# Node-by-edge selections on VectorE: 32-bit output in two edge walks, another element order in layer 2's first pass

## The chip, the cores and the metric

The kernel runs on one core of one Trainium2 chip. Its time is the device time of one execution in microseconds; the median of three executions is compared.

## What is computed

Four graph layers run one after the other over 6250 nodes of 128 features and 100000 edges sorted by destination. Each layer normalises the nodes, passes messages along the edges and adds its result to the nodes.

```python
h = jnp.maximum(_layernorm(x, axis=-1), 0.0);  x = x + _L0_gnn_ref(h, edge_attr_128, src, dst, ...)   # sums over edges
h = jnp.maximum(_layernorm(x, axis=-1), 0.0);  x = x + _L1_gnn_ref(h, edge_index, ...)                # attention, 8 heads
h = jnp.maximum(_layernorm(x, axis=-1), 0.0);  x = x + _L2_gnn_ref(h, edge_index, edge_type_8, ...)   # two relational layers
h = jnp.maximum(_layernorm(x, axis=-1), 0.0);  x = x + _L3_gnn_ref(h, edge_index, ...)                # attention, 2 heads
# attention, per edge: w = q[dst] . k[src];  softmax over the edges of a dst;  agg[dst] += softmax(w) * v[src]
# relational: mean over the edges of one dst and relation of (x @ W[relation])[src], summed over the 8 relations
```

## The kernel before

**Tiles and windows.** The nodes form 50 windows of 128. The sorted edges form up to 832 tiles of 128 edges, each of which belongs to one window; 829 tiles can hold edges. 16 tiles make a step, 52 steps a walk, and 4 tiles a group. `local_d` in DRAM holds, for every edge place, the number of its node inside its window.

**The selection.** From those numbers VectorE makes, for 16 tiles at once, a matrix of nodes by edges: partition n, column (tile, edge) is 1 where the edge's node is n. `make_selt` compares the 2048 numbers, broadcast to all partitions by one DMA on SP's queue, with the partition's own number `g.tile_f[:, 0:1]` (line 1874 in the walks, line 2793 in layer 2's first pass). Numbers and result are bf16; both are double-buffered by step.

**The two attention walks** (layers 1 and 3, `attention_edges`; tiles named l1te and l3te). ScalarE copies the bf16 selection into the 32-bit tile `wide` (`widen`, line 1784), which TensorE uses as weights in `look_up` (line 1671) to fetch each edge's query from its window. VectorE multiplies the queries with gathered rows (`product`), reduces them to scores, runs scans for the segment maximum, weighs the gathered values (`weigh`), and adds the tile sums that TensorE makes with a second selection (`sum_up`, line 1723) to the windows (`add`). Each engine has one written-out order per step: VectorE calls `make_selt(s + 1)` in the middle of step s, between two additions and ahead of `scan_carries`; TensorE looks up groups of step s + 1 at the end of step s; the weighing of a group comes two to three steps after its product.

**The gathers.** GpSimd issues one indirect DMA per tile (line 1627), which brings 128 rows of keys and values from `pair_d`. 48 buffers stand ready; a group of gathers waits for the weighing of 48 tiles before.

**Layer 2's first pass** (`gather_relations`; tiles named l2e). GpSimd gathers a tile of message rows (line 2644, 16 buffers). In `count` (line 2715) TensorE multiplies each tile's 128x128 slice of the selection, as weights, with the inverse counts of its window; from that VectorE makes a coefficient for each edge, and with it, per tile, the matrix for the sums of line 2762.

The last pass of layer 2 (`gather_nodes`; tiles named l2f, gathers in line 854) has no such selection. Nor has layer 0.

Of the kernel before, what the change touches and what calls it, by code (L numbers as in the profile page):

```python
# [5 lines left out]
P = 128  # L6
# [14 lines left out]
S = 16  # L21
NS = T // S
# [7 lines left out]
BF16 = mybir.dt.bfloat16  # L30
I32 = mybir.dt.int32
ALU = mybir.AluOpType
# [1522 lines left out]
def attention_edges(nc, g, sem, name, heads, queries, first, acc, aw, outputs=None):  # L1555
# [4 lines left out]
    GS = S // G  # L1560
# [9 lines left out]
    with Stage(nc, name) as st:  # L1570
        o = outputs(st) if late else None
        rows = g.xh[:, 0:R * 2 * D].rearrange("p (r f) -> p r f", f=2 * D)
        local = st.sb("local", [P, 2, S * P], BF16)
        selt = st.sb("selt", [P, 2, S, P], BF16)
        wide = st.sb("wide", [P, 2, S, P])
        sel = st.sb("sel", [P, V, G, P])
        narrow = st.sb("narrow", [P, 2, P, G], BF16)
# [28 lines left out]
        gathered = [sem(f"{name}_g{r}") for r in range(RG)]  # L1606
        local_in = [sem(f"{name}_local{b}") for b in range(2)]
        mask_in = [sem(f"{name}_mask{b}") for b in range(2)]
        (set_up, selt_made, widened, looked, used, reduced, sel_made, scores_turned, scanned, spread, summarised, carried,
         handed, picked, picked_sum, joined, topped, fell, shifted, firsts, expd, alphad, diagd, ex_turned, alpha_spread,  # L1610
         factored, scaled, weighted, beside, summed, added, taken, chosen, ready, cleared) = (
            sem(f"{name}_{k}") for k in (
                "set_up", "selt", "widened", "looked", "used", "reduced", "sel", "scturn", "scanned", "spread", "summar",
                "carried", "handed", "picked", "picksum", "joined", "topped", "fell", "shifted", "firsts", "expd", "alphad",
                "diagd", "exturn", "alspread", "factored", "scaled", "weighted", "beside", "summed", "added", "taken", "chosen", "ready", "cleared"))

# [3 lines left out]
        with nc.Block() as block:  # L1620
# [9 lines left out]
            @block.sync  # L1630
            def _(sp):
                if late:
                    o.load(sp)
                    o.fetch(sp, 0)
                    o.fetch(sp, 1)
                for s in range(NS):
                    b = s % 2
                    if s >= 2:
                        sp.wait_ge(selt_made, s - 1)
                    sp.dma_start(local[:, b, :], g.local_d[s * S * P:(s + 1) * S * P].partition_broadcast(P)) \  # L1640
                        .then_inc(local_in[b], 16)
                    if s >= 2:
                        sp.wait_ge(fell, s - 1)
                        if first:
                            sp.wait_ge(firsts, s - 1)
                    sp.dma_start(mask[:, b, :, :].rearrange("p k e -> p (k e)"), g.mask_d[s * P:(s + 1) * P, :]) \
                        .then_inc(mask_in[b], 16)
                    sp.dma_start(ends[:, b, :, :], view(g.ends_d.tensor, s * S, [[0, HS], [TA, 2], [1, S]])) \
                        .then_inc(mask_in[b], 16)
                    if late and s >= LAG + 2:  # L1650
                        o.store(sp, s - LAG - 2)
                        o.fetch_after(sp, s - LAG - 2)
                if late:
                    for k in range(NS - LAG - 2, o.EACH):
                        o.store(sp, k)
                        o.fetch_after(sp, k)
                    o.land(sp)
# [119 lines left out]

            @block.scalar
            def _(act):
                def widen(s):  # L1780
                    act.wait_ge(selt_made, s + 1)
                    if s >= 2:
                        act.wait_ge(looked, GS * (s - 1))
                    nc.scalar.copy(wide[:, s % 2, :, :], selt[:, s % 2, :, :]).then_inc(widened, 1)

                def exps(b):
                    act.wait_ge(fell, b + 1)
                    if b >= 1:
                        act.wait_ge(diagd, b)
                    nc.scalar.activation(alpha[:, :], fall[:, :], ACT.Exp).then_inc(alphad, 1)  # L1790
                    act.wait_ge(shifted, b + 1)
                    if b >= 1:
                        act.wait_ge(ex_turned, b)
                    nc.scalar.activation(ex[:, :], low[:, :], ACT.Exp).then_inc(expd, 1)
                    act.wait_ge(alphad, b + 1)
                    if b >= 1:
                        act.wait_ge(alpha_spread, b)
                    nc.scalar.activation(diag[:, 0:HS], g.ident[0:HS, 0:HS], ACT.Copy, scale=alpha[:, 0:1]).then_inc(diagd, 1)

                def take_weights(b):  # L1800
                    act.wait_ge(ex_turned, b + 1)
                    act.wait_ge(alpha_spread, b + 1)
                    if b >= 2:
                        act.wait_ge(beside, GS * (b - 1))
                    kinds = 2 if first else 1
                    nc.scalar.copy(weights[:, b % 2, 0:kinds, :, :], px[b % 2][:, 0:kinds, :, :]).then_inc(taken, 1)

                def widen_choice(n):
                    act.wait_ge(chosen, n + 1)
                    if n >= V:  # L1810
                        act.wait_ge(summed, G * (n - V + 1))
                    nc.scalar.copy(sel[:, n % V, :, :], narrow[:, n % 2, :, :].rearrange("p n t -> p t n")).then_inc(sel_made, 1)  # L1812

                def put_beside(n):
                    b = n // GS
                    act.wait_ge(taken, b + 1)
                    if n >= V:
                        act.wait_ge(summed, G * (n - V + 1))
                    k = n % GS * G
                    if first:  # L1820
                        ins = nc.scalar.copy(ve[:, n % V, :, D:].rearrange("p i (k h) -> p i k h", k=2),
                                             weights[:, b % 2, :, k:k + G, :].rearrange("p k i h -> p i k h"))
                    else:
                        ins = nc.scalar.copy(ve[:, n % V, :, D:], weights[:, b % 2, 0, k:k + G, 0:heads])
                    ins.then_inc(beside, 1)

                act.wait_ge(set_up, 1)
                widen(0)
                for j in range(5):
                    lo, hi = j * NW // 5 * aw, (j + 1) * NW // 5 * aw  # L1830
                    nc.scalar.activation(acc[:, lo:hi].rearrange("p (w f) -> p w f", f=EACH),
                                         g.iota[:, 0:EACH].unsqueeze(1).broadcast_to([P, (hi - lo) // EACH, EACH]),
                                         ACT.Copy, scale=0.0).then_inc(cleared, 1)
                for s in range(NS + 3):
                    b, z, y, k = s - 1, s - 2, s - 3, s - LAG
                    if late and k >= 1:
                        o.squash(act, k - 1)
                    if y >= 0:
                        widen_choice(GS * y + 3)
                        put_beside(GS * y + 3)  # L1840
                    if 0 <= z < NS:
                        widen_choice(GS * z)
                        for j in range(3):
                            put_beside(GS * z + j)
                    if s + 1 < NS:
                        widen(s + 1)
                    if 0 <= z < NS:
                        widen_choice(GS * z + 1)
                    if late and k >= 0:
                        o.share(act, k)  # L1850
                        o.move(act, k)
                        o.shift(act, k)
                    if 0 <= z < NS:
                        widen_choice(GS * z + 2)
                    if 0 <= b < NS:
                        exps(b)
                        take_weights(b)
                if late:
                    o.squash(act, NS + 2 - LAG)
                    for k in range(NS + 3 - LAG, o.EACH):  # L1860
                        o.share(act, k)
                        o.move(act, k)
                        o.shift(act, k)
                        o.squash(act, k)

            @block.vector
            def _(dve):
                windows = {}

                def make_selt(s):  # L1870
                    dve.wait_ge(local_in[s % 2], 16 * (s // 2 + 1))
                    if s >= 2:
                        dve.wait_ge(widened, s - 1)
                    nc.vector.tensor_scalar(selt[:, s % 2, :, :].rearrange("p s e -> p (s e)"), local[:, s % 2, :],
                                            g.tile_f[:, 0:1], None, ALU.is_equal).then_inc(selt_made, 1)

                def choose(n):
                    if n >= 2:
# [723 lines left out]
def gather_relations(nc, g, sem, name, table, index, width, acc, a):  # L2602
# [7 lines left out]
    with Stage(nc, name) as st:  # L2610
# [27 lines left out]
        with nc.Block() as block:  # L2638
# [147 lines left out]
            def _(dve):  # L2786
                c = Chain(dve, dv)

                def make_selt(s):
                    dve.wait_ge(local_in[s % 2], 16 * (s // 2 + 1))  # L2790
                    if s >= 2:
                        dve.wait_ge(counted, s - 1)
                    nc.vector.tensor_scalar(selt[:, s % 2, :, :].rearrange("p s e -> p (s e)"), local[:, s % 2, :],
                                            g.tile_f[:, 0:1], None, ALU.is_equal).then_inc(selt_made, 1)

                def mark(s):
# [197 lines left out]
```

## Time and profile before

| | us |
|---|---|
| median of 3 runs | 6016.26 (6013.54 to 6016.91) |
| the profiled execution | 6008.73 |
| its span, first to last instruction | 6006.7 |
| busy: TensorE / VectorE / GpSimd / ScalarE | 4143.8 / 3868.2 / 4039.4 / 1476.3 |
| mean granted TensorE clock, of full speed | 0.756 |
| gathers: walk 1, layer 2's first pass, its last pass, walk 2 begin at about | 1257, 2708, 3795, 4870 |

PE is TensorE's multiplication, PEld its weight load, DVE is VectorE, ACT ScalarE, POOL GpSimd. A busy share is a mean over stages with different limits, so each stage is read by itself: which engine has no idle time but its own issue, and which wait ends last. In the timeline two instructions of different engines can be set side by side by their start times.

### The profile page before, as it was taken

Reading aid. Unit: us, or ns where it says so; the run is one execution under the profiler, and the core shown is the slowest. Engines: PE = TensorE matmul, PEld = TensorE weight load, DVE = VectorE, ACT = ScalarE, POOL = GpSimd, SP = SyncE. Lnnn points to the kernel's source line nnn. Section 1 sums busy time; section 2 is a strip of 40 time slices with the busy share of each in tenths; the row PEclk is TensorE's granted clock in tenths of the full one; section 3 lists DMA queues with packets and bytes.
Section 4 is the critical chain, followed back from the end, with each engine's and each line's share of the span. In section 5 each row is a group of like instructions: output and inputs, shape, how many; then the busy total and the mean of one; then the engine's idle time right before and its main releaser. Section 6 shows DMA issues by size and latency. Waiting matters only on the chain. (4 is left out here: it accounts for less than half of the span.)

```text
span 6006.7 us, 86021 instructions
## 1 busy us (share of the span) xinstructions
PE 4143.8 (69%) x19030; PEld 3329.8 (55%) x19030; DVE 3868.2 (64%) x11925; ACT 1476.3 (25%) x3938; POOL 4039.4 (67%) x4191
## 2 busy tenths in 40 slices
PE   5678878867777766896878777444444447777776
PEld 4667766656666664444555555333333336666665
DVE  8555555557777777646666666344444447778885
ACT  5122222222222222451111111011111123333332
POOL 2677777757777774007777777577777767777773
PEclk9988888867777776998888888555555567777776
DMA  2544444434444445165454555222222254454443
GB/s 59 145 129 120 117 121 117 120 112 134 134 139 135 138 135 127 58 289 161 153 161 153 156 157 141 61 64 69 63 69 63 69 114 139 143 150 143 144 150 64
DMA packets 426774, 738.44 MB, mean 123 GB/s; under 512 B 100522, under 2 KB 280579, under 8 KB 419700
## 3 DMA queue, kind: packets, MB, share of 16 engines
q0 software_dynamic: 173200, 436.47, 27.6%
q1 hardware_dynamic: 244484, 289.62, 14.7%
q10 hardware_dynamic: 8592, 6.82, 0.4%
q8 instruction: 176, 2.88, 0.2%
q14 instruction: 322, 2.64, 0.1%
HBM read 613.55 MB, written 120.20 MB: 122 GB/s over the span
## 5 line engine op out<-in xcount | busy, mean ns | idle before, releaser
L1627 POOL DMA_INDIRECT xh<-pair_d,src_i x1658 | 1605.5, 968 | 570.6 <-issue 489.0
L2644 POOL DMA_INDIRECT l2e_rows<-msg_d,msg_i x829 | 798.3, 963 | 565.9 <-POOLq L61 313.7
L854 POOL DMA_INDIRECT l2f_rows<-msg_d,msg_i x829 | 785.3, 947 | 288.5 <-issue 241.1
L999 POOL DMA_INDIRECT l0e_rows<-node_d,src_i x829 | 786.7, 949 | 260.6 <-issue 218.3
L1156 PE MATMUL l0e_ps<-l0e_rows,l0e_sel 128*128 128x256 f32 x1664 | 671.6, 494 | 227.7 <-DVE early_acc L1223 90.0
L888 PE MATMUL l2f_ps<-l2f_rows,l2f_sel 128*128 128x128 f32 x1664 | 428.5, 424 | 578.1 <-DVE l2f_sel L907 366.5
L888 PEld LDWEIGHTS l2f_ps<-l2f_rows,l2f_sel 128*128 128x128 f32 x1664 | 373.4, 316 | 660.5 <-DVE l2f_sel L907 406.9
L2762 PE MATMUL l2e_ps<-l2e_rows,l2e_sel 128*128 128x256 f32 x1664 | 534.4, 447 | 187.4 <-DMA l2e_rows<-msg_d,msg_i 145.0
L919 DVE TENSOR_TENSOR xh<-xh,l2f_ps 128x128 f32 x832 | 239.5, 288 | 517.3 <-PE l2f_ps L888 410.6
L1223 DVE TENSOR_TENSOR early_acc<-early_acc,l0e_ps 128x264 f32 x832 | 356.8, 429 | 323.6 <-PE l0e_ps L1157 245.7
L2821 DVE TENSOR_TENSOR l_acc<-l_acc,l2e_ps 128x256 f32 x832 | 349.4, 420 | 304.3 <-PE l2e_ps L2762 300.7
L2762 PEld LDWEIGHTS l2e_ps<-l2e_rows,l2e_sel 128*128 128x128 f32 x1664 | 329.1, 218 | 337.0 <-issue 178.3
L1671 PE MATMUL l1te_pq<-l1t_queries,l1te_wide 128*128 x1664 | 332.2, 362 | 262.9 <-DVE l1te_prod L1890 252.2
L1671 PE MATMUL l3te_pq<-l3t_queries,l3te_wide 128*128 x1664 | 322.2, 354 | 256.4 <-DVE l3te_prod L1890 236.5
L1156 PEld LDWEIGHTS l0e_ps<-l0e_rows,l0e_sel 128*128 128x128 f32 x1664 | 310.7, 230 | 269.1 <-issue 211.5
L1671 PEld LDWEIGHTS l1te_pq<-l1t_queries,l1te_wide 128*128 128x128 f32 x1664 | 287.2, 260 | 309.8 <-issue 309.5
L1671 PEld LDWEIGHTS l3te_pq<-l3t_queries,l3te_wide 128*128 128x128 f32 x1664 | 279.1, 254 | 296.4 <-issue 294.8
L1157 PEld LDWEIGHTS l0e_ps<-l0e_of_rel,l0e_sel 128*128 128x128 f32 x1664 | 386.4, 232 | 74.2
L1723 PE MATMUL l1te_ps<-l1te_ve,l1te_sel 128*128 128x144 f32 x1664 | 373.2, 383 | 11.0 <-DVE l1te_ve L2003 10.8
L2019 DVE TENSOR_TENSOR l1acc_acc<-l1acc_acc,l1te_ps 128x144 f32 x832 | 246.8, 297 | 175.9 <-PE l1te_ps L1723 169.5
L1723 PEld LDWEIGHTS l1te_ps<-l1te_ve,l1te_sel 128*128 128x128 f32 x1664 | 326.5, 270 | 19.6 <-DVE l1te_ve L2003 13.5
L2019 DVE TENSOR_TENSOR l_acc<-l_acc,l3te_ps 128x130 f32 x832 | 234.4, 282 | 155.7 <-PE l3te_ps L1723 151.6
(454 smaller groups left out, 8074.5 us busy)
## 6 DMA issues: line engine op xcount, KB each, us to landing
l0e_rows<-in_edge_attr_dram SPq DMA_DIRECT2D x832, 64.0 KB
msg_d<-l1t_queries SPq DMA_DIRECT2D x50, 1024.0 KB, 3.9
l1te_local<-local_d SPq DMA_DIRECT2D x52, 512.0 KB, 4.8
l2e_local<-local_d SPq DMA_DIRECT2D x52, 512.0 KB
l3te_local<-local_d SPq DMA_DIRECT2D x52, 512.0 KB
xh<-pair_d,src_i POOLq DMA_INDIRECT x1658, 2.8
msg_d<-l2e_msg SPq DMA_DIRECT2D x50, 512.0 KB
l0e_rows<-node_d,src_i POOLq DMA_INDIRECT x829
```

Source lines behind the costliest of these rows:

```text
L854: pool.indirect_dma_start(rows[:, t % R, :], None, table, bass.IndirectOffsetOnAxis(index[:, t:t + 1], 0)) \
L888: nc.tensor.matmul(ps[t % B][:, 0:D], sel[:, n % V, t % G, :], rows[:, t % R, :], start=True, stop=True).then_inc(summed, 1)
L999: pool.indirect_dma_start(rows[:, t % R, 0:D], None, table, bass.IndirectOffsetOnAxis(g.src_i[:, t:t + 1], 0)).then_inc(gathered[t % R], 16)
L1156: nc.tensor.matmul(ps[r % B][:, 0:2 * D], sel[:, r // G % 2, r % G, :], rows[:, r, :], start=True, stop=True)
L1157: nc.tensor.matmul(ps[r % B][:, 2 * D:W0], sel[:, r // G % 2, r % G, :], of_rel[:, r // G % 2, r % G, :], start=True, stop=True).then_inc( ...
L1223: nc.vector.tensor_tensor(one, one, ps[s][:, 0:W0], ALU.add).then_inc(added, 1)
L1627: pool.indirect_dma_start(rows[:, t % R, :], None, g.pair_d, bass.IndirectOffsetOnAxis(g.src_i[:, t:t + 1], 0)).then_inc(gathered[n % RG], 16)
L1671: mm = nc.tensor.matmul(pq[n % 2][:, i * D:(i + 1) * D], wide[:, n // GS % 2, n % GS * G + i, :], queries[:, bass.ds(ws[i] * D, D)], start ...
L1723: nc.tensor.matmul(slot(t), sel[:, n % V, t % G, :], ve[:, n % V, t % G, :], start=True, stop=True).then_inc(summed, 1)
L2019: nc.vector.tensor_tensor(part, part, slot(t), ALU.add).then_inc(added, 1)
L2644: pool.indirect_dma_start(rows[:, t % R, :], None, table, bass.IndirectOffsetOnAxis(index[:, t:t + 1], 0)).then_inc(gathered[t % R], 16)
L2762: nc.tensor.matmul(ps[t % B][:, 0:width], sel[:, t // G % 2, t % G, :], rows[:, t % R, :], start=True, stop=True).then_inc(summed, 1)
```

## The change

In the walks the bf16 tile `selt`, its semaphore and ScalarE's `widen` go. VectorE's comparison writes `wide`, the 32-bit tile, itself, and waits for the lookups that last read that half of `wide`. SP's refill of the edge numbers waits for the same instruction as before, by the semaphore that it now raises. In layer 2's first pass the comparison keeps its tiles, types and place; only the order in which the 2048 columns are read and written changes, from edges inside tiles to tiles inside edges.

```diff
@@ attention_edges
-        selt = st.sb("selt", [P, 2, S, P], BF16)
         wide = st.sb("wide", [P, 2, S, P])
@@ sync
                     if s >= 2:
-                        sp.wait_ge(selt_made, s - 1)
+                        sp.wait_ge(widened, s - 1)
@@ scalar
-                def widen(s):
-                    act.wait_ge(selt_made, s + 1)
-                    if s >= 2:
-                        act.wait_ge(looked, GS * (s - 1))
-                    nc.scalar.copy(wide[:, s % 2, :, :], selt[:, s % 2, :, :]).then_inc(widened, 1)
...
-                widen(0)
...
-                    if s + 1 < NS:
-                        widen(s + 1)
@@ vector
                 def make_selt(s):
                     dve.wait_ge(local_in[s % 2], 16 * (s // 2 + 1))
                     if s >= 2:
-                        dve.wait_ge(widened, s - 1)
-                    nc.vector.tensor_scalar(selt[:, s % 2, :, :].rearrange("p s e -> p (s e)"), local[:, s % 2, :],
-                                            g.tile_f[:, 0:1], None, ALU.is_equal).then_inc(selt_made, 1)
+                        dve.wait_ge(looked, GS * (s - 1))
+                    nc.vector.tensor_scalar(wide[:, s % 2, :, :].rearrange("p s e -> p (s e)"), local[:, s % 2, :],
+                                            g.tile_f[:, 0:1], None, ALU.is_equal).then_inc(widened, 1)
@@ gather_relations, make_selt
-                    nc.vector.tensor_scalar(selt[:, s % 2, :, :].rearrange("p s e -> p (s e)"), local[:, s % 2, :],
+                    nc.vector.tensor_scalar(selt[:, s % 2, :, :].rearrange("p s e -> p e s"),
+                                            local[:, s % 2, :].rearrange("p (s e) -> p e s", s=S),
                                             g.tile_f[:, 0:1], None, ALU.is_equal).then_inc(selt_made, 1)
```

## Rows read from the trace of the kernel before

**Rows 1.** Busy time by stretch: PE, PEld, DVE, ACT, POOL, clock, DMA share, GB/s

```profile
1260.00:2320.00 1060.00, 744.74 (x3781) 656.80 (x3782) 805.76 (x2443) 301.98 (x655) 802.17 (x827) 0.73 0.48 135
2700.00:3760.00 1060.00, 828.91 (x3477) 569.05 (x3476) 691.13 (x1954) 133.93 (x340) 798.31 (x829) 0.86 0.52 155
4870.00:5930.00 1060.00, 750.20 (x4144) 670.60 (x4144) 815.31 (x2622) 344.68 (x878) 795.50 (x824) 0.76 0.50 143
```

**Rows 2.** GpSimd's waits, whole span: total us, times, longest us

```profile
POOL xh L1627 <- issue: 489.0, 1605, 0.3
...
POOL l2e_rows L2644 <- issue: 228.4, 750, 0.3
...
POOL l2e_rows L2644 <- PE l2e_ps L2762: 23.8, 78, 0.3
```

**Rows 3.** The page's groups: count, busy us, mean ns, idle before

```profile
L1627 POOL DMA_INDIRECT xh<-pair_d,src_i x1658 | 1605.5, 968 | 570.6 <-issue 489.0
L2644 POOL DMA_INDIRECT l2e_rows<-msg_d,msg_i x829 | 798.3, 963 | 565.9 <-POOLq L61 313.7
L854 POOL DMA_INDIRECT l2f_rows<-msg_d,msg_i x829 | 785.3, 947 | 288.5 <-issue 241.1
```

**Rows 4.** Waits for gathered rows: 1400 to 2200, 5000 to 5800, 2900 to 3600

```profile
DVE l1te_prod L1890 <- DMA xh<-pair_d,src_i: 40.1, 51, 3.6
...
DVE l3te_prod L1890 <- DMA xh<-pair_d,src_i: 45.8, 37, 2.6
...
PE l2e_ps L2762 <- DMA l2e_rows<-msg_d,msg_i: 96.6, 48, 4.0
```

**Rows 5.** Timeline, five places: start us, duration us, engine, line

```profile
1943.42 0.95 POOL L1627 DMA_INDIRECT xh<-pair_d,src_i  x1 [0.30 <-issue]
1943.43 0.75 DVE L1874 TENSOR_SCALAR l1te_selt<-l1te_local,tile_f 128x2048 bf16<-128x2048 bf16 x1
...
1474.58 1.32 POOL L1627 DMA_INDIRECT xh<-pair_d,src_i  x1 [0.30 <-issue]
1475.03 0.75 DVE L1874 TENSOR_SCALAR l1te_selt<-l1te_local,tile_f 128x2048 bf16<-128x2048 bf16 x1
...
2249.01 0.95 POOL L1627 DMA_INDIRECT xh<-pair_d,src_i  x1 [0.30 <-issue]
2249.50 0.97 DVE L1874 TENSOR_SCALAR l1te_selt<-l1te_local,tile_f 128x2048 bf16<-128x2048 bf16 x1
2250.27 1.02 POOL L1627 DMA_INDIRECT xh<-pair_d,src_i  x1 [0.30 <-issue]
...
1575.66 0.95 POOL L1627 DMA_INDIRECT xh<-pair_d,src_i  x1 [0.30 <-issue]
1576.76 0.75 DVE L1874 TENSOR_SCALAR l1te_selt<-l1te_local,tile_f 128x2048 bf16<-128x2048 bf16 x1
1576.92 1.41 POOL L1627 DMA_INDIRECT xh<-pair_d,src_i  x1 [0.31 <-issue]
...
2874.53 0.94 POOL L2644 DMA_INDIRECT l2e_rows<-msg_d,msg_i  x1 [0.30 <-issue]
2875.67 0.75 DVE L2793 TENSOR_SCALAR l2e_selt<-l2e_local,tile_f 128x2048 bf16<-128x2048 bf16 x1
2875.78 1.45 POOL L2644 DMA_INDIRECT l2e_rows<-msg_d,msg_i  x1 [0.30 <-issue]
```

**Rows 6.** Selection and copy: ns min/median/max, first and last start; who waited, us, times

```profile
L1874 DVE TENSOR_SCALAR l1te_selt<-l1te_local,tile_f x52: 744/748/999, 1259.9 to 2292.8; 128x2048 bf16<-128x2048 bf16 x52
...
L1784 ACT CAST l1te_wide<-l1te_selt x52: 1897/1898/1902, 1261.0 to 2293.7; 128x2048 f32<-128x2048 bf16 x52
...
  PE l3te_pq L1671: 19.5, 2
  PE l1te_pq L1671: 10.5, 1
```

**Rows 7.** Single-input VectorE work of two widths, grouped: busy us, mean ns

```profile
L447 DVE CAST od_lows<-iota 125x2048 bf16<-125x2048 f32 x1 | 1.2, 1200 | 0.0
...
L478 DVE CAST tb_local<-tb_rawf 128x896 bf16<-128x896 f32 x1 | 1.1, 1086 | 0.0
```

More of the change, by code:

```diff
@@ L1608, in attention_edges @@
         mask_in = [sem(f"{name}_mask{b}") for b in range(2)]
-        (set_up, selt_made, widened, looked, used, reduced, sel_made, scores_turned, scanned, spread, summarised, carried,
+        (set_up, widened, looked, used, reduced, sel_made, scores_turned, scanned, spread, summarised, carried,
          handed, picked, picked_sum, joined, topped, fell, shifted, firsts, expd, alphad, diagd, ex_turned, alpha_spread,
@@ L1612, in attention_edges @@
             sem(f"{name}_{k}") for k in (
-                "set_up", "selt", "widened", "looked", "used", "reduced", "sel", "scturn", "scanned", "spread", "summar",
+                "set_up", "widened", "looked", "used", "reduced", "sel", "scturn", "scanned", "spread", "summar",
                 "carried", "handed", "picked", "picksum", "joined", "topped", "fell", "shifted", "firsts", "expd", "alphad",
```

## The prediction

> **What bounds the kernel now.** I read the busy table by stretch first [rows 1]. In all three stages that the change touches no engine is busy all the time: GpSimd stands at 0.75 of each stretch, VectorE at 0.65 to 0.77, TensorE at 0.71 to 0.78. So the table alone names no bound. GpSimd's own waits do [rows 2]: before nearly every gather it stood idle for 0.30 us on "issue", that is on nothing but its own instruction stream, and 0.30 us was also all that it waited where a semaphore came last. The gathers of a stage therefore follow one another without a hole: 968 ns mean and 0.30 us between them [rows 3] make 1.27 us, times 829 tiles is 1055 us, and the windows of 1060 us in rows 1 hold just that. GpSimd's gathers set the pace of both walks and of layer 2's first pass, a step of 16 tiles every 20.3 us.
>
> The others keep up with little to spare [rows 4]. In the steady part of walk 1 VectorE stood 40.1 us for gathered rows in 39 steps of 20.3 us, 1.0 us a step; in walk 2 (layer 3) 45.8 us in 39 steps, 1.2 us. In layer 2's pass TensorE stood 96.6 us for rows in 35 steps, 2.8 us a step. These are what a step may grow on VectorE before VectorE's loop takes over from the gathers.
>
> What can move the time is thus the length of a gather, and it does vary. An undisturbed gather takes 0.945 us; the means are 968 in the walks, 963 in layer 2's pass and 947 in the stage that has no selection (L854) [rows 3]. The timeline shows who stretches it [rows 5]. Let p be how long after the start of the running gather a selection (L1874 or L2793) starts; gathers start 1.25 us apart.
> - p 0.01: the selection ends at 0.76 and the gather keeps its 0.95.
> - p 0.45: it ends at 1.20 and the gather takes 1.32, 0.37 more.
> - p 0.49: now the selection waits. It takes 0.97 instead of 0.75, and the next gather takes 1.02, 0.07 more.
> - p 1.10 (past the gather's end): the next gather takes 1.41, 0.46 more. In layer 2's pass, p 1.14 gives 1.45.
>
> So a gather has two places at which it needs something that this VectorE instruction holds until its end; who comes first has it, and the other waits. In numbers that fit these rows: a selection that starts at p up to 0.46 delays the running gather by (its end - 0.83), if positive; one between 0.46 and 0.71 is itself held until 0.71; from there to 1.11 it delays the next gather by (its end - 1.38); in the last 0.14 us it waits for the next gather's start and then falls under the first case. With starts spread evenly over 1.25 us and 0.748 us of selection, the mean is (0.072 + 0.019 + 0.110) / 1.25 = **0.16 us** a selection. The 104 of the walks make 17 us of the 1658 x 0.023 = 38 us by which their gathers exceed 0.945; the rest belongs to other VectorE work, which stays.
>
> **The change part by part.**
>
> *Walks: the ScalarE copy goes.* 104 casts of 1.90 us leave ScalarE [rows 6]. TensorE waited for one only three times, 30.0 us in all, at the two starts, while gathers ran regardless; ScalarE is 0.28 to 0.33 busy [rows 1]. I cost it at nothing: the gathers hide it. Without that cover it would be worth at most the 30.0 us. VectorE's new wait (the lookups of two steps before) is already met, since the products ahead of it in VectorE's order wait for later lookups; behind it stand the carry scans and the additions, which do not move for it. SP's refill of the edge numbers now waits for the same instruction's new semaphore, so it comes later by its growth only.
>
> *Walks: the selection writes 32 bits.* The trace has no bf16 to f32 selection. The nearest row is a VectorE cast over 2048 columns between 32 and 16 bits, 1.20 us [rows 7], two columns a cycle (2048 / 2 at 0.96 GHz is 1.067 us, the 0.96 from selections: 748 ns is 512 cycles, 0.533 us, and 0.215 us fixed). With the selection's fixed part: 1.067 + 0.215 = 1.28 us, 0.53 more on VectorE per step. That is under the 1.0 us that a step has to spare. For the gathers the same rule at 1.28 us gives (0.46 x 0.68 + 0.25 x 0.61 + 0.40 x 0.81 + 0.14 x 0.45) / 1.25 = 0.68 us, 0.52 more than now. **104 x 0.52 = +54 us.** Bounds: below, -17 us, if the new form held nothing of the gather's; above, 104 x 0.60 = +62 us, since a longer hold can add no more than its own growth and a few missed starts.
>
> *Layer 2's pass: tiles inside edges.* Reading and writing now step 128 bf16 elements (256 bytes) from one column to the next. No row of the trace has such a step on VectorE. Ends: 1.28 us (two columns a cycle as in the cast) and 2.35 us (one a cycle, 2.133 + 0.215; the trace has single-input copies at that rate, 128x896 in 1086 ns, where the row structure of both sides differs [rows 7]). Neither row has the step, so I take the middle, 1.82 us. At such lengths the rule gives nearly the length less 0.60: 1.22 us against 0.16, **52 x 1.06 = +55 us**; at 1.28 it is 52 x 0.52 = +27, at 2.35 52 x 1.59 = +83, and -8 us if nothing is held. VectorE's 1.07 us more a step lies inside the 2.8 us to spare. TensorE reads the same tile as before.
>
> The trace says nothing of what a step of 256 bytes costs on VectorE. The Trainium skill does (Vector Engine (DVE) Microarchitecture Reference, 5.2 Measured stream behaviour on trn2): a port keeps full rate only over pairs of adjacent 4-byte words, and streams that hop at each element took 1.7 to 2.5 ns a column there. As an estimate, 1024 such columns on two ports would be 2.0 to 2.8 us for this selection, and the total 6132 to 6173 us; no run here shows it.
>
> **Sum.** The profiled execution's 6008.7 us (span 6006.7 and 2.0 around it) + 54 + 55 = 6118 us. The median of the runs is 7.5 us above the profiled one; the same +109 us on it gives **6125 us**. With the ends of the second term, 6097 to 6153.
>
> **The rivals.**
> 1. *The stepped selection no longer holds the gathers (or is turned back into the old order).* A selection at one column a cycle that works through one port would stand beside the gathers without touching them. For it: the 1086 ns copy [rows 7] shows that the slower rate exists for single-input work. Against: there it comes from row structures that differ, and here both sides have the same. VectorE's 1.6 us more stays inside 2.8 us. Time: walks +54, pass -8: 6062 us; 6070 if the order is unchanged. The Trainium skill speaks both ways: VectorE: DVE Perf Modes, "Mode 1x (REGULAR) - the baseline", counts odd strides among what falls back to that mode, while "What auto-detection actually checks" asks of the two-port mode only even outer counts and SBUF.
> 2. *Neither holds them: not slower.* If the 32-bit output too drops to one column a cycle without the hold, the gathers win 17 + 8 = 25 us: 5991 us. The price is 1.60 us of VectorE a step in the walks. The point from which it decides is the 1.0 us to spare plus the 0.16 of the lost stretch: beyond that 0.4 us a step, up to 104 x 0.4 = +45 us, comes back unless VectorE's waits for TensorE's sums take it up. Against it: the 1.20 us cast mixes both widths at two columns a cycle [rows 7].
> 3. *ScalarE's cast was on the path.* If the walks were held by the look-up chain, taking 1.90 us out of each step would show; at most the 30.0 us of waits [rows 6], 5986 us even if the selections cost nothing. The 0.30 us gaps [rows 2] speak against it.
>
> **How the numbers follow.** Forecast 0.62; rival 1 0.25; rival 2 0.08; rival 3 0.02; 0.03 for something slower than all. The range takes in the forecast's own span, rival 1, and above 6153 the growth that a step dearer than one column a cycle would bring (another 0.4 us x 52 = 21 us): 6050 to 6175. A measurement of this kernel tells about 0.2%, 12 us, from no change. Slower by more: forecast, rival 1, half of rival 2's returned cost and the rest, 0.88; faster 0.07; same 0.05.
>
> **What would show it.** Right: L1874 at about 1.28 us in both walks; the gathers' mean there from 968 to about 1000 ns (104 x 0.52 us over 1658), still 0.30 us apart; L2793 near 1.8 us and that pass's gathers from 963 to about 1030; the stages without a selection unchanged. VectorE's waits for rows should remain. Wrong: selections of 2.2 us or more beside gathers of 0.945, VectorE's waits for rows gone and GpSimd waiting for VectorE, or selections of the forecast length with unchanged gathers.

## The result, and the profile after

The changed kernel takes 6259.99 us (median of 5, 6250.78 to 6264.59) against 6013.54 us before: a ratio of 1.0411, 95% interval 1.0398 to 1.0423. It is slower, as forecast, but by 246 us and not by 109, and outside the range. Of its profiled executions' spans, 6248.9 against 6006.7 us, 242 us have to be found.

Two of the three stretches after, walk 1 and layer 2's first pass (the columns of [rows 1]; each stage has grown, so the windows are longer):

```profile
1260.00:2350.00 1090.00, 748.58 (x3797) 659.27 (x3797) 835.04 (x2450) 208.91 (x603) 827.09 (x827) 0.73 0.47 131
2735.00:3980.00 1245.00, 864.32 (x3477) 582.95 (x3478) 881.28 (x1952) 134.15 (x340) 988.68 (x829) 0.84 0.44 130
```

Walk 1 went from about 1060 to 1090 us, layer 2's pass from about 1060 to 1245. The groups of gathers (answering to [rows 3]; their lines are 1626, 2634 and 854 now) say in what:

```profile
L1626 POOL DMA_INDIRECT xh<-pair_d,src_i x1658 | 1656.1, 999 | 569.9 <-issue 484.7
L2634 POOL DMA_INDIRECT l2e_rows<-msg_d,msg_i x829 | 988.7, 1193 | 568.9 <-POOLq L61 316.6
L854 POOL DMA_INDIRECT l2f_rows<-msg_d,msg_i x829 | 785.3, 947 | 290.9 <-issue 239.5
```

1658 x (999 - 968) ns = 51 us in the walks and 829 x (1193 - 963) ns = 191 us in the pass: 242 us, the whole difference. The stage without a selection stands where it stood. GpSimd's waits (answering to [rows 2]) have kept their 0.30 us, so what has changed on GpSimd is the gathers' own length:

```profile
POOL xh L1626 <- issue: 484.7, 1591, 0.3
POOL l2e_rows L2634 <- POOLq L61: 316.6, 1, 316.6
POOL l2e_rows L2634 <- issue: 239.8, 787, 0.3
```

The selections (answering to [rows 6]; ns min/median/max):

```profile
L1864 DVE TENSOR_SCALAR l1te_wide<-l1te_local,tile_f x52: 1271/1279/1520, 1260.8 to 2317.8; 128x2048 f32<-128x2048 bf16 x52
...
L2783 DVE TENSOR_SCALAR l2e_selt<-l2e_local,tile_f x52: 4815/4832/4996, 2740.7 to 3940.3; 128x2048 bf16<-128x2048 bf16 x52
```

The 32-bit one takes the forecast 1.28 us. The one with tiles inside edges takes **4.83 us**, 6.5 times its old 0.75, where 1.82 was forecast and 2.35 was the upper end. The timeline shows the same hold as in [rows 5], only longer; one place of walk 2 and two of the pass:

```profile
5703.52 0.95 POOL L1626 DMA_INDIRECT xh<-pair_d,src_i  x1 [0.30 <-issue]
5704.47 1.28 DVE L1864 TENSOR_SCALAR l3te_wide<-l3te_local,tile_f 128x2048 f32<-128x2048 bf16 x1
5704.77 1.80 POOL L1626 DMA_INDIRECT xh<-pair_d,src_i  x1 [0.30 <-issue]
...
3632.49 0.97 POOL L2634 DMA_INDIRECT l2e_rows<-msg_d,msg_i  x1 [0.30 <-issue]
3633.57 4.83 DVE L2783 TENSOR_SCALAR l2e_selt<-l2e_local,tile_f 128x2048 bf16<-128x2048 bf16 x1
3633.76 4.95 POOL L2634 DMA_INDIRECT l2e_rows<-msg_d,msg_i  x1 [0.30 <-issue]
...
3561.89 4.97 DVE L2783 TENSOR_SCALAR l2e_selt<-l2e_local,tile_f 128x2048 bf16<-128x2048 bf16 x1
3562.61 4.57 POOL L2634 DMA_INDIRECT l2e_rows<-msg_d,msg_i  x1 [0.30 <-issue]
```

In the first, p is 0.95 and the rule gives 0.95 + 1.28 - 1.38 = 0.85 us; the gather takes 0.85 more than 0.95. In the pass a gather that takes 0.95 us elsewhere takes 4.95 or 4.57 here; over the whole pass 52 gathers take more than 3 us, one for each of the 52 selections, and the others keep a median of 0.946. VectorE's waits for gathered rows in the walks are unchanged, 42.9 us in walk 1 between 1400 and 2200 (answering to [rows 4]): the gathers still set the pace.

```profile
DVE l1te_prod L1880 <- DMA xh<-pair_d,src_i: 42.9, 41, 3.2
```

So the mechanism of the forecast holds, and one duration in it does not. The experiments ask three things: do the two parts add up by themselves; is it the hold of the gathers or the length on VectorE that costs; and what makes the stepped selection take 4.83 us.

### The profile page after: what moved, and what is told of

Its sections match the earlier page's. It is cut to its first block and busy times, and to the rows that moved or that the text cites. A ratio compares the mean times of both kernels' runs of the same rounds, so it can differ in the third digit from the quotient of the medians.

```text
span 6248.9 us, 85815 instructions
## 1 busy us (share of the span) xinstructions
PE 4216.3 (67%) x19030; PEld 3374.9 (54%) x19030; DVE 4114.4 (66%) x11925; ACT 1296.7 (21%) x3834; POOL 4282.0 (69%) x4191
## 5 line engine op out<-in xcount | busy, mean ns | idle before, releaser
L1626 POOL DMA_INDIRECT xh<-pair_d,src_i x1658 | 1656.1, 999 | 569.9 <-issue 484.7
L2634 POOL DMA_INDIRECT l2e_rows<-msg_d,msg_i x829 | 988.7, 1193 | 568.9 <-POOLq L61 316.6
L1156 PE MATMUL l0e_ps<-l0e_rows,l0e_sel 128*128 128x256 f32 x1664 | 706.7, 517 | 199.4 <-DVE early_acc L1223 88.3
L2752 PE MATMUL l2e_ps<-l2e_rows,l2e_sel 128*128 128x256 f32 x1664 | 555.6, 457 | 336.9 <-DVE l2e_sel L2847 164.3
L1156 PEld LDWEIGHTS l0e_ps<-l0e_rows,l0e_sel 128*128 128x128 f32 x1664 | 328.2, 242 | 232.6 <-issue 174.4
L1157 PEld LDWEIGHTS l0e_ps<-l0e_of_rel,l0e_sel 128*128 128x128 f32 x1664 | 407.0, 245 | 83.1
L1722 PE MATMUL l3te_ps<-l3te_ve,l3te_sel 128*128 128x130 f32 x1664 | 324.5, 350 | 13.7 <-DVE l3te_ve L1993 9.7
```

What stands on the lines that cost most here:

```text
L1156: nc.tensor.matmul(ps[r % B][:, 0:2 * D], sel[:, r // G % 2, r % G, :], rows[:, r, :], start=True, stop=True)
L1157: nc.tensor.matmul(ps[r % B][:, 2 * D:W0], sel[:, r // G % 2, r % G, :], of_rel[:, r // G % 2, r % G, :], start=True, stop=True).then_inc( ...
L1626: pool.indirect_dma_start(rows[:, t % R, :], None, g.pair_d, bass.IndirectOffsetOnAxis(g.src_i[:, t:t + 1], 0)).then_inc(gathered[n % RG], 16)
L1722: nc.tensor.matmul(slot(t), sel[:, n % V, t % G, :], ve[:, n % V, t % G, :], start=True, stop=True).then_inc(summed, 1)
L2634: pool.indirect_dma_start(rows[:, t % R, :], None, table, bass.IndirectOffsetOnAxis(index[:, t:t + 1], 0)).then_inc(gathered[t % R], 16)
L2752: nc.tensor.matmul(ps[t % B][:, 0:width], sel[:, t // G % 2, t % G, :], rows[:, t % R, :], start=True, stop=True).then_inc(summed, 1)
```

## The experiments

### Each part by itself

The theory is that a selection holds the running or the next gather until the selection ends, so that each part costs its own growth. The rival is that the two cost only together.

```diff
# e1_walks_alone: the changed kernel, with layer 2's selection as before
-  nc.vector.tensor_scalar(selt[...].rearrange("p s e -> p e s"), local[...].rearrange("p (s e) -> p e s", s=S), ...)
+  nc.vector.tensor_scalar(selt[...].rearrange("p s e -> p (s e)"), local[:, s % 2, :], ...)
# e2_pass_alone: the kernel before, with the opposite edit
```

> The change in the walks alone; layer 2's first pass as before. If the hold of the gathers is what costs, and each part by itself: selections of 1.28 us in both walks, gathers there at a mean of 999 ns, +50 us against before (1658 x 0.031), ratio 1.008; layer 2's pass unchanged at 963 ns. If the rival holds, that the two parts cost only together (say through TensorE's clock or the buffers' place), the sum of this and the other half is not the whole +246 us.

> The change in layer 2's first pass alone; both walks as before. If the hold is what costs: selections of 4.83 us, that pass's gathers at a mean of 1193 ns, +190 us against before (829 x 0.230), ratio 1.032, walks unchanged at 968 ns. If the parts cost only together, less than that.

Walks alone: 6060.71 against 6010.59 us, ratio 1.0086 (1.0071 to 1.0101), +50 us. Layer 2's pass alone: 6206.9 against 6010.59, ratio 1.0326 (1.0310 to 1.0342), +196 us. The groups of gathers, of the first run and then of the second:

```profile
L1626 POOL DMA_INDIRECT xh<-pair_d,src_i x1658 | 1660.5, 1001 | 568.6 <-issue 486.8
L2634 POOL DMA_INDIRECT l2e_rows<-msg_d,msg_i x829 | 797.3, 962 | 568.2 <-POOLq L61 316.0
```

```profile
L1627 POOL DMA_INDIRECT xh<-pair_d,src_i x1658 | 1610.9, 972 | 568.7 <-issue 486.2
L2644 POOL DMA_INDIRECT l2e_rows<-msg_d,msg_i x829 | 994.8, 1200 | 569.4 <-POOLq L61 317.2
```

Each run stretches the gathers of its own stage and leaves the other's alone, and 50 + 196 is the whole 246 us. The rival falls.

### Hold or length

In layer 2's pass the same comparison was made by the instruction's form that also sums its outputs (the sum is not used): once in the old order, once with tiles inside edges.

```diff
# e6_accum: the kernel before, layer 2's selection (e9_accum_step: the same with the changed kernel's two access orders)
-                                            g.tile_f[:, 0:1], None, ALU.is_equal).then_inc(selt_made, 1)
+                                            g.tile_f[:, 0:1], None, ALU.is_equal, ALU.add,
+                                            accum_out=unused[:, s % 2:s % 2 + 1]).then_inc(selt_made, 1)
```

> The kernel before, but layer 2's selection is made by the form of the same instruction that also adds up its outputs (the sum is not used), in the old order. In layer 0 that form ran at one column a cycle. Expected 2.3 to 2.4 us, three times the 0.75 of before. If it is the hold and not the length that costs, and this form holds nothing: gathers in that pass at some 948 to 955 ns instead of 963, 8 us less in all, ratio 0.999; VectorE's 1.6 us more a step lies inside the 2.8 us to spare. If the length on VectorE costs: gathers still 0.30 us apart but delayed by missing sums, up to 52 x 1.6 = +83 us. If this form holds the gathers too: a mean of about 1050 ns and +80 us.

> The same form with the changed kernel's order (tiles inside edges) in layer 2's pass. It separates length from hold: VectorE is kept as long as in the changed kernel or about so (4 to 5 us, if a single column a cycle pays for the step too). If the hold is the cause: gathers at some 950 ns, and the time is set by VectorE's 3.3 to 4.3 us more against 2.8 us to spare, so 0 to 52 x 1.5 = +78 us, with GpSimd waiting for TensorE's sums. If the length is the cause: as the change in that pass alone, +196 us.

In the old order: 6007.75 against 6015.25 us, ratio 0.9986 (0.9976 to 0.9995), although the selection is three times as long. Its selection and its gathers:

```profile
L2793 DVE TENSOR_SCALAR_CACHE_REDUCE l2e_selt<-l2e_local,tile_f x52: 2333/2340/2345, 2717.1 to 3720.4; 128x2048 bf16<-128x2048 bf16 x52
```

```profile
L2644 POOL DMA_INDIRECT l2e_rows<-msg_d,msg_i x829 | 788.7, 951 | 570.3 <-POOLq L61 318.1
```

2.34 us on VectorE beside gathers of 951 ns, 12 less than before: 1.6 us more of length alone costs nothing there, and without the hold the gathers win back what the old selection took. With tiles inside edges this form takes 9.36 us and the kernel 6279.99 us, ratio 1.0440 (1.0423 to 1.0458), dearer than the change. But not through the gathers. Its timeline at one selection, its group of gathers, and GpSimd's waits for TensorE's sums up to 3760 (the pass goes on to about 4030):

```profile
3000.69 9.36 DVE L2793 TENSOR_SCALAR_CACHE_REDUCE l2e_selt<-l2e_local,tile_f 128x2048 bf16<-128x2048 bf16 x1
3000.91 0.95 POOL L2644 DMA_INDIRECT l2e_rows<-msg_d,msg_i  x1 [0.30 <-issue]
3002.17 0.95 POOL L2644 DMA_INDIRECT l2e_rows<-msg_d,msg_i  x1 [0.30 <-PE l2e_ps L2762]
3002.30 1.88 PE L2747 MATMUL l2e_pm<-l2e_w,l2e_ht 128*128 128x512 f32 x4
...
3003.42 0.95 POOL L2644 DMA_INDIRECT l2e_rows<-msg_d,msg_i  x1 [0.30 <-issue]
...
3009.68 0.43 DVE L2858 TENSOR_SCALAR l2e_sel<-iota,dloc,coef 128x128 f32<-128x128 f32 x1
...
3011.96 2.08 PE L2762 MATMUL l2e_ps<-l2e_rows,l2e_sel 128*128 128x256 f32 x4 [7.35 <-DVE l2e_sel L2858]
...
3013.83 3.58 PE L2747 MATMUL l2e_pm<-l2e_w,l2e_ht 128*128 128x512 f32 x4
...
3018.55 0.94 POOL L2644 DMA_INDIRECT l2e_rows<-msg_d,msg_i  x1 [6.70 <-PE l2e_ps L2762]
```

```profile
L2644 POOL DMA_INDIRECT l2e_rows<-msg_d,msg_i x829 | 785.3, 947 | 849.1 <-POOLq L61 316.3
```

```profile
POOL l2e_rows L2644 <- PE l2e_ps L2762: 240.8, 74, 7.2
```

Gathers of 0.95 us run straight through a selection of 9.36 us; then GpSimd stands 6.70 us until TensorE's sums free a buffer. That is the other bound, VectorE's loop. VectorE starts its next work 8.99 us after the selection's start (3009.68), against 0.66 in the old order (median of 52): 8.3 us more a step. Of that the kernel shows 264.7 / 52 = 5.1 us a step, as idle time of GpSimd: 849.1 us before this group of gathers against 565.9 in the kernel before, 283 more, less 13 us by which the gathers are shorter. Not all of the 5.1 need be VectorE's own: after it had stood 7.35 us, TensorE took 3.58 us for what took 1.88 at 3002.30, at a granted clock of 0.56 of full speed between 3012.0 and 3017.9, that is mostly at the lower of its two levels, 1.2 GHz; it was 1.00 between 3000 and 3004. The expected 4 to 5 us of length was wrong, and with it the expected 0 to 78 us; the two signs that tell hold from length came as the hold has them. In the changed kernel, once its first gather has started, GpSimd has no wait above 0.3 us in that pass: the 4.1 us more that its selection takes on VectorE show in the stretched gathers alone.

The Trainium skill (SBUF — State Buffer, "Who interferes with whom") states that VectorE's two-port modes and GpSimd exclude each other for the whole instruction, and counts the form that writes out its accumulator as one that cannot enter them. The gathers of 947 ns beside it, and of 1193 beside the plain form, agree. The whole instruction is a little too long for stepped writing, where the next gather came free about half a microsecond before the selection's recorded end, as the section on the prediction shows.

### What makes the step dear

All in layer 2's pass of the kernel before, except the last. If two columns go at once, one through each port, (duration - 0.215 fixed) / 1024 is the price of such a pair; the 0.215 us is the forecast's figure.

```diff
# e3_step_read: only the reading steps;  e4_step_write: only the writing
+ selt[...].rearrange("p s e -> p (s e)").rearrange("p (e s) -> p e s", s=S),  local[...].rearrange("p (s e) -> p e s", s=S)
+ selt[...].rearrange("p s e -> p e s"),                                       local[...].rearrange("p (e s) -> p e s", s=S)
# e5_step16, e5b_step2: both step, by b = 16 or 2 elements
+ selt[...].rearrange("p s e -> p (s e)").rearrange("p (a b) -> p b a", b=b),  local[...].rearrange("p (a b) -> p b a", b=b)
# e10_wide_step: the changed kernel's walks with the stepped order, layer 2's pass as before
+ wide[...].rearrange("p s e -> p e s"),                                       local[...].rearrange("p (s e) -> p e s", s=S)
```

> The kernel before, but in layer 2's pass the selection reads with the step of 256 bytes and writes its columns one after another (so TensorE's slices hold the columns in another order and that layer's coefficients are not the reference's). Three cases for the 4.83 us of the stepped selection (4.62 us beside 0.215 fixed, 4.5 ns for each pair of columns): the reading side alone pays, then 4.8 us here; the writing side alone, then 1.3 us here; both pay alike and it adds up, then about 3.1 us. The gathers' mean in that pass follows the length less some 0.7 to 0.95 us: 1193, 980 or 1085 ns.

> The counterpart: it reads one after another and writes with the step of 256 bytes (again the columns land in another order and that layer's coefficients are not the reference's). Reading alone pays: 1.3 us here; writing alone: 4.8 us; both alike: about 3.1 us. If neither half alone is dear and only both together are, both runs show 1.3 to 2 us.

> The kernel before with both sides of layer 2's selection stepped alike, by 16 elements (32 bytes) in place of 128 (256 bytes). If what costs is any step that leaves the neighbouring word: 4.8 us as with 128. If the distance counts (256 bytes meeting the same place again and again): clearly less, down to the 1.28 us of two columns a cycle.

> The same with a step of 2 elements (4 bytes). The columns are then neighbouring words and only no longer neighbouring 16-bit elements: if leaving the neighbouring word is what costs, 1.28 us here, the price of two columns a cycle without a packed pair, and gathers at some 980 ns in that pass; if any step other than one costs, 4.8 us.

> The changed kernel's walks with the 32-bit selection written and read in the order tiles inside edges (512 bytes from one output column to the next), layer 2's pass as before. In the pass, writing 16-bit columns with a step cost 4.5 ns for each pair of columns and reading with one 1.73 ns. If the writing pays because a 16-bit column is less than a word, 32-bit columns pay about what the reading does: some 2 us a selection, gathers of the walks at about 1045 ns, some +75 us over the walks' 1001. If any stepped writing pays 4.5 ns: 4.8 us a selection, gathers at 1190 ns or so, some +310 us, unless VectorE's loop (3.6 us more a step against 1.0 to spare) takes over first, which gives about the same.

The selections of the five, in that order:

```profile
L2793 DVE TENSOR_SCALAR l2e_selt<-l2e_local,tile_f x52: 1952/1987/2101, 2712.6 to 3784.9; 128x2048 bf16<-128x2048 bf16 x52
```

```profile
L2793 DVE TENSOR_SCALAR l2e_selt<-l2e_local,tile_f x52: 4773/4792/4992, 2719.3 to 3920.6; 128x2048 bf16<-128x2048 bf16 x52
```

```profile
L2793 DVE TENSOR_SCALAR l2e_selt<-l2e_local,tile_f x52: 4586/4744/4865, 2715.7 to 3915.0; 128x2048 bf16<-128x2048 bf16 x52
```

```profile
L2793 DVE TENSOR_SCALAR l2e_selt<-l2e_local,tile_f x52: 1412/1436/1650, 2716.2 to 3761.9; 128x2048 bf16<-128x2048 bf16 x52
```

```profile
L1864 DVE TENSOR_SCALAR l1te_wide<-l1te_local,tile_f x52: 2292/2542/2616, 1263.3 to 2376.4; 128x2048 f32<-128x2048 bf16 x52
```

| access | us | ns per pair | gathers' mean, ns | kernel, us |
|---|---|---|---|---|
| 32-bit written, none steps (the change's walks) | 1.28 | 1.04 | 999 | - |
| both step 4 bytes | 1.44 | 1.19 | 1004 | 6042 |
| reading steps 256 bytes | 1.99 | 1.73 | 1036 | 6069 |
| 32-bit written, both step | 2.54 | 2.27 | 1067 (walks) | 6176 |
| both step 32 bytes | 4.74 | 4.42 | 1192 | 6199 |
| writing steps 256 bytes | 4.79 | 4.47 | 1195 | 6209 |
| both step 256 bytes (the change's pass) | 4.83 | 4.51 | 1193 | 6260 (with its walks) |

The kernel times but the last are single executions beside 6007 to 6012 us of the kernel before. Writing 16-bit columns that lie 32 bytes or more apart is what costs, 4.4 to 4.5 ns for each on its port; the reading goes on beside it. The distance hardly matters from 32 to 256 bytes, and at 4 bytes nearly all is gone. A stepped 32-bit column (512 bytes apart) costs half of a 16-bit one. Three expectations were too low: reading alone took 1.99 us for 1.3, the step of 4 bytes 1.44 for 1.28, the stepped 32-bit columns 2.54 for some 2. In the form through one port above, (9358 - 215) / 2048 = 4.46 ns a column: the same price, for twice as many columns one after another. That also shows that the changed selection did use both ports, and that the step has not thrown it back to one, as the first rival had it. Why a 16-bit column is twice as dear as a 32-bit one is not shown; that a word has to be kept in part is only a thought.

### Shorter holds

If the hold is the cause, cutting a selection into pieces lets the gathers in between.

```diff
# e7_halves (n = 2, kernel before, both stages);  e8_wide_quarters (n = 4 on wide in the changed walks, 2 in the pass, old order);
# e11_quarters_accum (kernel before: n = 4 on selt in the walks, the pass as in e6_accum)
+  for q in range(n):
+      lo, hi = q * S // n, (q + 1) * S // n
+      ins = nc.vector.tensor_scalar(selt[:, s % 2, lo:hi, :].rearrange("p s e -> p (s e)"), local[:, s % 2, lo * P:hi * P],
+                                    g.tile_f[:, 0:1], None, ALU.is_equal)
+  ins.then_inc(selt_made, 1)
```

> The kernel before, with each bf16 selection of 2048 columns made by two instructions of 1024, in both walks and in layer 2's pass. The rule of the hold (delay of the running gather = end of the instruction - 0.83 us, of the next = end - 1.38 us) gives 0.02 us for an instruction of 0.48 us against 0.16 us for one of 0.75: each selection stretches the gathers by some 0.05 us in all, 156 x 0.11 = 17 us less, about 5996 us, ratio 0.997; gathers of the walks at a mean of about 961 ns. VectorE works 0.21 us more a step. Rival: two instructions back to back hold on as one does (the waiting gather doesn't get in between): then 0.96 us of hold, gathers stretched more than now, about +0.2 us x 156 = +30 us.

> The changed kernel's walks, but the 32-bit selection in four instructions of 512 columns (0.48 us each, 1.9 us in all), and layer 2's pass with its old order in two halves. By the rule of the hold, 0.02 us of stretch per piece: the gathers win 17 us in the walks' two and the pass together, less what four pieces keep (104 x 0.09 = 9 us): about 6005 us, ratio 0.998, if VectorE's 1.2 us more a step stays beside the gathers (1.0 to 1.2 us were to spare). If VectorE's loop takes over instead: up to 104 x 0.2 us = 20 us slower than that, its waits for gathered rows gone. If pieces hold on as one: slower than the change in the walks alone.

> A version after these findings: the kernel before, with the walks' bf16 selection in four instructions of 512 columns (0.35 us each), and layer 2's in the summing form that holds nothing. By the rule of the hold the walks lose nearly all of the 0.16 us a selection (gathers from 968 to about 958 ns, 17 us) and the pass some 10 us (951 ns): about 27 us less, ratio 0.9955. VectorE's 0.64 us more a step in the walks lies inside the 1.0 us to spare; if it doesn't, its waits for gathered rows are gone and the ratio is near 1.

Halves: 5998.05 against 6010.59 us, ratio 0.9982 (0.9973 to 0.9991); the walks' gathers at the expected 961 ns, those of the pass at 956. The gathers are 12 and 6 us shorter, the expected 17 in all; of that 12.5 us came out in the time, so the ratio is a little above the expected 0.997.

```profile
L1627 POOL DMA_INDIRECT xh<-pair_d,src_i x1658 | 1593.4, 961 | 571.1 <-issue 490.2
```

Quarters of the 32-bit selection: 6014.79 against 6010.59 us, ratio 1.0006 (0.9997 to 1.0015), where 0.998 was expected. Gathers of its walks and VectorE's waits for rows between 1400 and 2200:

```profile
L1626 POOL DMA_INDIRECT xh<-pair_d,src_i x1658 | 1612.8, 973 | 570.5 <-issue 496.0
```

```profile
DVE l1te_prod L1884 <- DMA xh<-pair_d,src_i: 0.7, 2, 0.4
```

Cutting removed most of the 50 us that the 32-bit output had cost the walks (999 to 973 ns), but four pieces of 0.48 us in a row keep 1658 x (973 - 958) / 104 = 0.24 us a selection where the rule gave 0.09; 958 is the mean without a selection's part by the rule (968 ns less 17 us over 1658). And VectorE's waits for rows are gone, 0.7 us from 40.1: its 1.2 us more a step have used up just the 1.0 us that [rows 4] gave as spare. Nothing in this run shows a gain from the copy that ScalarE no longer makes.

Quarters of the bf16 selection in the walks and the summing form in the pass: 5986.42 against 6012.32 us, ratio 0.9958 (0.9944 to 0.9972), faster than both kernels, with the gathers where the rule put them:

```profile
L1627 POOL DMA_INDIRECT xh<-pair_d,src_i x1658 | 1587.1, 957 | 572.0 <-issue 489.0
L2648 POOL DMA_INDIRECT l2e_rows<-msg_d,msg_i x829 | 787.4, 950 | 570.1 <-POOLq L61 317.8
```

## Why the prediction was right and wrong

**What bounds the kernel: right.** The 242 us lie wholly in the gathers' length, with their gaps at 0.30 us.

**The hold: right.** The rule read from five places of the timeline gave 0.52 us more a selection at 1.28 us; the walks' 51 us are 51 / 104 = 0.49. It also placed the halves (961 ns, as expected) and the quarters of bf16 (957 against 958). Over both walks of the changed kernel it is off by 2 to 4 ns at the median: 28 selections that start up to 0.46 us after a gather's start, and 39 that start from 0.71 to 1.11 after it. It is too high for the changed selection of the pass: 4.83 - 0.60 - 0.16 = 4.07 us was to be expected more per selection, and 191 / 52 = 3.67 came. The timeline shows where: in the second case (p 1.08) the gather now ends 0.31 us after the selection (3638.71 and 3638.40), where it ended 0.82 us after it in the 32-bit selection (5706.57 and 5705.75). So it is in all 21 places of that pass with p from 0.71 to 1.11 (median 0.31), and in the run that steps the writing alone (0.31, 15 places). Where only the reading steps the gather ends 0.83 us after the selection, as the rule has it, and at 1.99 us the rule is still right: the difference goes with stepped writing and not with length. For p up to 0.46 the rule is off by 0.05 us only. VectorE's own next instruction, too, starts 0.39 us before the recorded end of the stepped selection (median; 3638.01 in the second case) and 0.08 before that of the 32-bit one. So part of it may be a recorded end that comes late when writing is stepped; the cause stays open.

**ScalarE's copy at nothing: right.** The walks alone lost 50 us where their gathers grew by 1658 x (1001 - 968) ns = 55 us, so at most some 5 us can have been won beside it.

**32-bit output, two columns a cycle: right,** 1.28 us; +54 forecast, +50 measured by itself.

**Tiles inside edges: the term that was mis-sized.** It was put at 1.82 us and +55 us and measured 4.83 us and +191 (+196 by itself). The failed step is the upper end: it took "one column a cycle" for the slowest rate there can be, from the row of a copy whose columns are neighbours in runs of 128, and took the middle between the two ends because no row had the step. A stepped 16-bit write runs at 4.3 cycles of 0.96 GHz a column on each port (4.51 ns). The sentence of the Trainium skill beside it (Vector Engine (DVE) Microarchitecture Reference, 5.2) gave the right direction and 2.0 to 2.8 us. Its 1.7 to 2.5 ns a column are of 32-bit streams: the 16-bit reading (1.73) and the 32-bit output (2.27) agree with it, the 16-bit writing (4.47) does not. Even by the upper end of that estimate the total would have stayed at 6173 us (6175 when the rule is worked out again). Had the row been 4.83, the same rule would have given 6016 + 54 + 52 x 4.07 = 6282 us, and 6261 with the 3.67 measured.

**VectorE's spare time: right in the walks** (1.0 us a step, used up by the quarters of the 32-bit selection), **and about right in the pass:** 2.8 us was read, and of the summing form's 8.3 us more a step all but 5.1, some 3.2, were taken up. With TensorE's slower stretches among the 5.1 it may be somewhat more.

**The rivals.** The first (the step ends the hold) is refuted by the timeline and by the price through one port. The second gave the right picture of a form that holds nothing, but the 32-bit output is not one; the summing form is. The third, at most 30 us of gain, fell with the walks alone: they are 50 us slower.

## What to carry to other kernels

When the gathers of one engine set the pace, look in the timeline for instructions of its neighbour beside each stretched gather: what such an instruction costs is the time from the gather's need to the instruction's end. Here a selection of 1.28 us or more paid nearly its whole growth, and pieces of 0.35 us next to nothing. Cutting it into short pieces, or using a form that holds nothing, gained here even though it lengthened VectorE's own work, as long as VectorE had time to spare; where that was used up (the quarters of the 32-bit selection) there was no gain over the kernel before. And an access order was not free: a bound taken from rows of neighbouring columns is no bound for a stepped one, and an unknown of that kind should be measured or given a far wider end.

## What the runs showed of the hardware beyond that

VectorE wrote 16-bit columns 32 or 256 bytes apart at 4.4 to 4.5 ns each per port, 4.3 times the price of neighbouring 32-bit ones (1.04), and 32-bit columns 512 bytes apart, with a stepped reading, at 2.27 ns. Reading with a step of 256 bytes cost 1.73 ns and disappeared beside the writing. The summing form of the comparison ran at one column a cycle in the old order (2.34 us for 2048) and at 4.46 ns a column in the stepped one, and let gathers pass at 951 and 947 ns.
